# Attention, then experts: later waits for stores, the last normalisation on VectorE, shorter ranks and lists, products of ones in TensorE's waits

## What is computed

```python
x = x + attention(layernorm(x), ctx)     # self (causal) and cross, 16 heads, projection Wp
z = layernorm(x)
# expert choice: each of 8 experts takes the 512 of all 4096 tokens with the highest score
scores = (jnp.tanh(z @ gate_w.T) + 1.0) * 0.5
vals, idx = jax.lax.top_k(scores.T, 512)
y = layernorm(z[idx]) * gamma + beta
o = gelu(y @ fc1s + b1s) @ fc2s + b2s    # one 256 -> 1024 -> 256 network for each expert
out = x + z.at[idx].add(o * vals)
```

## Time and profile before

| | |
|---|---|
| time, median of 3 runs | 1618.84 us (1618.71, 1618.84, 1629.46) |
| the profiled execution's own time | 1623.42 us |
| its span, first to last instruction | 1621.7 us |
| PE, DVE, ACT, POOL busy | 92%, 70%, 56%, 34% of the span |
| mean granted clock | 0.95 |
| attention | to 1260 us, tail to 1281 us |
| routing, first list and first gather | 1281 to 1352 us |
| eight experts | 1352 us to the end |

### The profile page before, as it was taken

How to read it: one execution, slowest core, us unless ns; L and a number is a source line. 1 busy time by engine, 2 the same in 40 slices (tenths; PEclk the granted TensorE clock), 3 DMA queues, 4 the chain that set the end, 5 groups by cost and what they waited for, 6 DMA issues and landing times. The chain is left out here.

```text
span 1621.7 us, 26374 instructions
## 1 busy us (share of the span) xinstructions
PE 1486.5 (92%) x8925; PEld 726.8 (45%) x8925; DVE 1135.0 (70%) x3163; ACT 911.5 (56%) x1754; POOL 550.1 (34%) x1005
## 2 busy tenths in 40 slices
PE   8899999999999999999999999999998336999897
PEld 4443443444444444444444344444344223655564
DVE  6868887877887788778778887877850374554441
ACT  2167777677676777776776777777766001121111
POOL 4122333442352334334423533441131202434342
PEclk9599999999999999999999999999999557999999
DMA  6776652855467466728564773666001201443332
GB/s 131 153 137 104 128 81 81 114 117 103 103 115 126 94 93 127 124 79 116 104 116 100 113 130 83 102 122 108 4 3 40 83 1 53 92 114 98 105 87 50
DMA packets 82491, 155.46 MB, mean 96 GB/s; under 512 B 13012, under 2 KB 46420, under 8 KB 82356
## 3 DMA queue, kind: packets, MB, share of 16 engines
q1 hardware_dynamic: 76212, 145.25, 46.4%
q0 software_dynamic: 6144, 8.52, 3.0%
HBM read 96.52 MB, written 53.08 MB: 92 GB/s over the span
## 5 line engine op out<-in xcount | busy, mean ns | idle before, releaser
L827 ACT ACTIVATE probs<-bank_ps 128x512 f32<-128x512 f32 (+1 forms) x1408 | 730.4, 579 | 247.2 <-PE bank_ps L616 238.5
L918 DVE TENSOR_REDUCE chunk_max<-bank_ps 128x1 f32<-128x512 f32 x1024 | 653.5, 683 | 143.4 <-PE bank_ps L655 139.6
L655 PE MATMUL bank_ps<-k_stack,q_stack 62*128 62x512 f32 (+3 forms) x1536 | 536.1, 432 | 7.7 <-DVE chunk_max L918 4.4
L616 PE MATMUL bank_ps<-q_stack,k_stack 64*128 64x512 f32 (+3 forms) x1536 | 511.7, 422 | 26.0 <-ACT probs L827 22.6
L655 PEld LDWEIGHTS bank_ps<-k_stack,q_stack 62*128 62x128 f32 x1536 | 248.2, 191 | 371.3 <-DVE chunk_max L918 201.6
L921 DVE CUSTOM_DVE_ANT_0 masked<-bank_ps,causal 128x128 bf16<-128x128 f32 (+3 forms) x512 | 232.9, 485 | 62.1 <-PE bank_ps L655 58.6
L634 PE MATMUL out_ps<-probs,v_cross 128*32 128x512 f32 x2048 | 274.3, 608 | 0.0
L616 PEld LDWEIGHTS bank_ps<-q_stack,k_stack 64*128 64x128 f32 x1536 | 234.5, 189 | 83.9 <-ACT probs L827 76.5
L1081 POOL TENSOR_TENSOR pool_idle<-pool_idle 128x1 f32<-128x1 f32 x293 | 56.8, 194 | 581.9 <-ACT probs L827 383.5
L1379 ACT ACTIVATE h<-h_ps,b1T 128x512 f32<-128x512 f32 x64 | 44.0, 688 | 270.0 <-PE h_ps L1332 270.0
L1346 PE MATMUL o_ps<-w2T,h 128*128 128x256 f32 x512 | 117.1, 386 | 13.8 <-ACT h L1379 7.0
(11 more groups left out here) (159 smaller groups left out, 1357.1 us busy)
## 6 DMA issues: line engine op xcount, KB each, us to landing
parts_dram<-parts SPq DMA_DIRECT2D x70, 512.0 KB, 2.8
k_stack<-parts_dram SPq DMA_DIRECT2D x180, 192.0 KB, 11.7
q_stack<-parts_dram SPq DMA_DIRECT2D x180, 128.0 KB, 10.6
w1T<-in_L_ffn_fc1s SPq DMA_DIRECT2D x8, 1024.0 KB, 5.7
w2T<-in_L_ffn_fc2s SPq DMA_DIRECT2D x8, 1024.0 KB, 7.6
z_rows<-z_sb SPq DMA_DIRECT2D x8, 528.0 KB, 3.1
x_sb<-in_x SPq DMA_DIRECT2D x8, 512.0 KB, 3.9
ctxT<-in_ctx SPq DMA_DIRECT2D x8, 512.0 KB, 4.8
```

The source lines that it names most:

```text
L616: mm = pe.matmul(bank_of(turn)[:, of.at:of.end], k_stack[base:base + SIDE, g, pair, of.keys:of.keys + P], q_stack[base:base + SIDE, g, pai ...
L655: return pe.matmul(bank[:, 0:n], q_stack[base:base + MAX_ROWS, g, pair, qc:qc + P], k_stack[base:base + MAX_ROWS, g, pair, k0:k0 + n], sta ...
L827: nc.scalar.activation(probs[:, buffer(u, i, p), side, columns], bank_of(("score", g, i, p, side))[:, columns], ACT.Exp, scale=SCALE)\
L918: nc.vector.tensor_reduce(dst, bank[:, 0:n], AX.X, ALU.max).then_inc(max_done, 1)
```

## The change

`MEANWHILE` names four pieces of the last batch's tail behind which TensorE multiplies `ones_row` by itself into a bank that nobody reads (one 32-bit product of 512 columns, or four). VectorE takes the statistics of the first two tiles as soon as `proj0` is added, and normalises the last batch itself; POOL only makes `rstd` and the sum. `stored` is gone from the end of attention: `x1`, `z_sb` and the two semaphores outlive the block, and POOL waits for the stores ahead of the first gather (`z_out`) and the second (`base_out`). In the second block TensorE no longer waits for `consts` ahead of the rounds, and multiplies ones by `warm` (16-bit, 512 columns) four times behind each round and 32 times behind the first list. The ranks are counted from one; a third product with minus ones takes the subtraction's place; the tied tokens' counts have a bank of their own and don't wait for `count`; the last round makes no new levels, `thr` and `e_place` are not copied, `not_first` is set by POOL. `list_head` has 6 instructions. Each tile of a gather has its own semaphore.

```diff
+MEANWHILE = {"out_self": 1, "yT1": 1, "proj1": 4, "zT1": 1}
...
                 piece(epilogue_piece(B - 1, n), epilogue_bank(n))
+                if name in MEANWHILE:
+                    multiply_ones(MEANWHILE[name])
...
+                if name in PROJ_PIECES:
+                    c = PROJ_PIECES.index(name)
+                    dve.wait_ge(proj_added, 2 * B - 1 + c)
+                    tile_stats(1, x1[:, 2 * c, :], 2 * c)
+                    st = tile_stats(1, x1[:, 2 * c + 1, :], 2 * c + 1)
                 if name == "proj1":
-                    dve.wait_ge(proj_added, 2 * B)
-                    norm_stats(1, lambda t: x1[:, t, :], B)
+                    st.then_inc(stats_done[1], 1)
+                    mean_and_var(1, B)
+                    normalize(1, lambda t: z_sb[:, t, 0:C], lambda t: x1[:, t, :], B)
...
+                if n < B - 1:
+                    normalize(1, lambda t: z_sb[:, t, 0:C], lambda t: x1[:, t, :], n + 1)
+                else:
+                    deviation(1, n + 1)
...
-            stored(B)
...
-            pe.wait_ge(consts, 3)
+            def multiply_ones(times):
+
+                for _ in range(times):
+                    pe.matmul(transpose_ps[:, 0], ones[:], warm[:], start=True, stop=True)
+
+            pe.wait_ge(pool_set, 1)
             for r in range(ROUNDS):
                 pe.wait_ge(tested, r + 1)
                 for t in range(0, TILES, TILE_STEP):
                     mm = pe.matmul(reached_ps, ones[:], reached[:, :, :, t:t + TILE_STEP], start=t == 0,
                                    stop=t == TILES - TILE_STEP)
                 mm.then_inc(counted, 1)
-
-            pe.wait_ge(route, 2)
-            pe.matmul(count_ps[:, 0, :], ones[:], above[:].rearrange("p e t -> p (e t)"), start=True, stop=True)\
+                multiply_ones(ONES_PER_ROUND)
+
+            pe.wait_ge(consts, 3)
+            pe.wait_ge(route, 1)
+            pe.matmul(above_ps, ones[:], above[:].rearrange("p e t -> p (e t)"), start=True, stop=True)\
                 .then_inc(route_ps, 1)
-            pe.wait_ge(route, 4)
-            for n, tile in enumerate((tied, chosen)):
+            for tile, step in ((tied, 2), (chosen, CHOSEN_STEP)):
                 flat = tile[:].rearrange("p e t -> p (e t)")
-                if n:
-                    pe.wait_ge(route, CHOSEN_STEP)
-                pe.matmul(count_ps[:, 0, :], upto[:], flat, start=True, stop=True)
-                pe.matmul(count_ps[:, 1, :], ones[:], flat, start=True, stop=True).then_inc(route_ps, 1)
+                pe.wait_ge(route, step)
+                pe.matmul(count_ps[:], ones[:], flat, start=True, stop=True).then_inc(route_ps, 1)
+                pe.matmul(ahead_ps, upto[:], flat, start=True, stop=False)
+                pe.matmul(ahead_ps, minus_ones[:], flat, start=False, stop=True).then_inc(route_ps, 1)
             list_products(0)
+            multiply_ones(ONES_BEFORE_ITEMS)
...
-                nc.vector.tensor_copy(e_place[:], place[:, e, :])\
+                at = place[:, e, :]
+                nc.vector.tensor_tensor(e_at[:], at.unsqueeze(1).broadcast_to([P, NT + 1, TILES]),
+                                        chunk_from[:].unsqueeze(2).broadcast_to([P, NT + 1, TILES]), ALU.is_ge)\
                     .then_inc(list_step, 1)
                 dve.wait_ge(list_step, s + 1)
-                for c in range(1, NT):
-                    st = nc.vector.tensor_scalar(e_col[:, c, :], e_place[:], c * P - 0.5, None, ALU.is_ge)
+                nc.vector.tensor_reduce(e_sum[:], e_at[:, 1:NT, :].rearrange("p c t -> p t c"), AX.X, ALU.add)\
+                    .then_inc(list_step, 1)
+                nc.vector.tensor_tensor(e_col[:], e_at[:, 0:NT, :], e_at[:, 1:NT + 1, :], ALU.subtract).then_inc(list_step, 1)
+                dve.wait_ge(list_step, s + 2)
+                nc.vector.scalar_tensor_tensor(out=e_row[:], in0=e_sum[:], scalar=-float(P), in1=at,
+                                               op0=ALU.mult, op1=ALU.add).then_inc(list_step, 1)
+                dve.wait_ge(list_step, s + 3)
+                for v in range(2):
+                    st = nc.vector.tensor_tensor(e_rhs[:, :, v, :], e_col[:].rearrange("p c t -> p t c"),
+                                                 token[:, v, :].unsqueeze(2).broadcast_to([P, TILES, NT]), ALU.mult)
                 st.then_inc(list_step, 1)
...
+                dve.wait_ge(list_step, s + LIST_STEPS)
...
-                dve.wait_ge(rows_in, 16 * NT * (e + 1))
                 for t in range(NT):
+                    dve.wait_ge(rows_in[t], 16 * e + 16)
                     st = nc.vector.bn_stats(stats[:, t, :], rows[:, t, 0:C])
...
-                nc.vector.tensor_tensor(levels[:], low[:].unsqueeze(1).broadcast_to([P, 1 + TESTS, E]), steps[:],
-                                        ALU.add).then_inc(round_step, 1)
-
-            nc.vector.tensor_copy(thr[:], low[:]).then_inc(route, 1)
-            dve.wait_ge(route, 1)
-            nc.vector.tensor_tensor(above[:], s_all[:], wide(thr), ALU.is_gt).then_inc(route, 1)
-            nc.vector.tensor_tensor(tied[:], s_all[:], wide(thr), ALU.is_equal).then_inc(route, 1)
+                if r < ROUNDS - 1:
+                    nc.vector.tensor_tensor(levels[:], low[:].unsqueeze(1).broadcast_to([P, 1 + TESTS, E]), steps[:],
+                                            ALU.add).then_inc(round_step, 1)
+
+            nc.vector.tensor_tensor(above[:], s_all[:], wide(low), ALU.is_gt).then_inc(route, 1)
+            nc.vector.tensor_tensor(tied[:], s_all[:], wide(low), ALU.is_equal).then_inc(route, 1)
             dve.wait_ge(route_ps, 1)
-            nc.vector.tensor_reduce(count[:], count_ps[:, 0, :].rearrange("p (e t) -> p e t", e=E), AX.X, ALU.add)\
+            nc.vector.tensor_reduce(count[:], above_ps.rearrange("p (e t) -> p e t", e=E), AX.X, ALU.add)\
-            dve.wait_ge(route, 4)
+            dve.wait_ge(route, 3)
...
-            nc.vector.memset(not_first[:], 1.0).then_inc(route, 1)
-            dve.wait_ge(route, 6)
-            nc.vector.memset(not_first[:, :, 0:1], 0.0).then_inc(route, 1)
-            dve.wait_ge(route, 7)
+            dve.wait_ge(consts, 3)
...
                 dve.wait_ge(route, step + 1)
-                nc.vector.tensor_tensor(flat(tmp), flat(scan), count_ps[:, 1, :], ALU.subtract).then_inc(route, 1)
+                dve.wait_ge(route_ps, n + 1)
+                nc.vector.tensor_tensor(flat(place), flat(scan), ahead_ps, ALU.add).then_inc(route, 1)
                 dve.wait_ge(route, step + 2)
-                nc.vector.tensor_tensor(flat(place), flat(tmp), count_ps[:, 0, :], ALU.add).then_inc(route, 1)
-                dve.wait_ge(route, step + 3)
-
...
-CHOSEN_STEP = 13
+CHOSEN_STEP = 9
+ONES_PER_ROUND = 4
+ONES_BEFORE_ITEMS = 32
...
+            pool.wait_ge(z_out, 16 * BATCHES)
             gather(0)
+            pool.wait_ge(base_out, 16 * BATCHES)
```

101 lines of the change are left out of this document (49 added, 52 removed).

## The result

The changed kernel takes **1597.23 us** (median, 1593.62 to 1601.58, 4 runs), the kernel before 1621.99 (1618.71 to 1629.46, 4 runs). The ratio is 0.984, 95% interval 0.981 to 0.987: 1.6% faster. A second series gave 1592.72 (1591.76 to 1597.13, 5 runs) against 1624.18, ratio 0.982 (0.979 to 0.985). The prediction was 1594.7.

A forecast was written before the change was run, and what follows sets the result against it. Bound: the 80 us chain of attention's tail, routing and first gather, one engine at a time; in the experts, TensorE's waits. Terms sum to 25.1, 24.1 for the median: 1618.8 to 1594.7 us, own range 1590 to 1598, with rivals to 1602.

The forecast's parts named there:

- A: Tail of attention: earlier statistics, normalisation on VectorE, transposes and gate at the high clock; 6.7 us saved.
- B: Stores at attention's end: next block starts 0.44 behind the last store's issue, not its landing; 3.6 us (3.2 to 3.9).
- C: First round of the routing: TensorE no longer waits for POOL's last iota; 0.8 us (0.4 to 0.9).
- D: Routing rounds: four products of ones in each wait raise the clock and shorten the counting; 3.6 us (0 to 4.8).
- mostly high with a fall now and then: Granted clock expected in the 13 routing rounds, the first two low; basis for 3.6 us.
- ceiling of 4.8: Routing rounds: most gain if counting fell from 0.82 to 0.45, 0.37 a round, in all 13.
- Rival 1: Clock doesn't hold in the rounds nor first products: rounds give 0 to 1, gain 20.5, 1598 us; chance 0.20.
- E: Ranks and lists, last `low` to first one-hot: fewer and narrower VectorE operations; 4.0 us (3.0 to 5.0).
- F: First gather: three of four tile statistics now lie before the last landing; 1.0 us (0.4 to 1.1).
- the wait moves to POOL and covers itself: Stores: their wait, moved ahead of the first gather some 60 us later, was to cost nothing.
- G: 32 products of ones ahead of expert 0's transposes: transposes and first products run high; 0.5 us (-2.1 to 2.4).
- H: Experts: statistics by tile shorten TensorE's waits for VectorE, 6.6 us in 5 waits; 4.9 us (0.5 to 5.8).

The follow-up runs named there:

- undoing B alone: Changed kernel with SyncE again waiting for the last batch's two stores at attention's end and POOL's two waits gone: 1596.5 us, ratio 0.982.
- both experiments: Changed kernel with one wait for all four gathered tiles, 1599.5 us; kernel before with only a semaphore for each gathered tile, 1617.2 us.
- the second execution of before: The kernel before, unchanged, profiled once more: 1616.8 us, with 266.4 from the first product to the end.
- both ways of removing it: Changed kernel with stores waited for in attention, 1596.5 us; changed kernel with more ones, bridged, and POOL's waits ahead of its last iota, 1591.1 us.

## Why the prediction was right, point by point

- **Tail, stores, first round (A, B, C)**: 11.1 predicted, 11.15 measured (23.41 less 12.26), and 3.6 of it undone by undoing B alone. Durations of like instructions elsewhere in the trace were good to 0.03 us (transposes 1.06 for 1.09, gate 1.92 for 1.95, normalisation 1.38). The low case given for A is a slip: 6.7 less 1.6 is 5.1 and not 4.9. Not in the sum: the products ahead of the projection may also stop a fall of the clock that comes in some executions.
- **Rounds (D)**: this term was too large. In the profiled execution "mostly high with a fall now and then" failed: nine of 13 counts ran low, and it gained 1.2. In five others with the same rounds it gained 1.2 once and 2.9 four times; there it held, with three or four counts low. With four ones, and TensorE idle for 3.4 us or more ahead of them, the first two to four rounds are low; later the clock falls once in three of the six executions, twice in two and not at all in one. The ceiling of 4.8 was too high as well: all 13 rounds high give 3.9, 0.30 each, since the count took 0.51 and not the 0.45 that the gate's ratio gave. The Trainium skill ("TensorE: Matmul & The Clock Gate", section "A second HAM failure mode: psum-queue depth-cycling"), which the prediction weighed there, states that short idles between groups of products make the clock swing. Five of the six traces with four ones agree with it in kind, 0.50 and 1.00 in turn; the sixth, high for 23 us with 1.17 idle in every round, does not. Half of the ceiling, 2.4, lies inside what came. Rival 1, which gave D 0 to 1, came near twice in six. With seven ones the idles are still there, 0.53 a round, and the clock does not swing.
- **Ranks and lists (E)**: 4.1 for 4.0. Counting operations by width, 0.42, 0.29 and 0.16, was enough.
- **First gather (F)**: 0.4 for 1.0. The saving of three statistics is there (1.0 by both experiments); "the wait moves to POOL and covers itself" failed in a term of 0.36: a wait that is long satisfied, placed directly ahead of the gather, made its issue late. Another 0.15 goes with the wide operations on VectorE beside POOL's step (0.33 and not 0.19); with the wait still in place, undoing them alone brought 0.13, and only from the second transfer on.
- **Products ahead of the transposes (G)**: not late, as said; the fall of the clock in the gap behind them was named and came around the transposes each time. 0.2 here, and 0.5 in expert 0 (counted in H above), where 0.5 was put for both; expert 0 alone varies by more than that (33.0 and 33.9 in the two executions of the changed kernel).
- **Experts (H)**: the mechanism (VectorE free for tile 0 sooner) was right, the size in the profiled executions was not: 9.0 for 4.9. Against the second execution of before it is 6.2, and 5.3 in the second of the changed kernel, which is near 4.9; 2.8 was the first execution's own chance. What the term left out: "counts where TensorE waited" is too narrow, as an expert in which no wait for `o` shows became 0.35 shorter as well. The low clock behind the longest wait did go, but it was not there in the second execution of before either, so the change can't be given those 0.9.

The median came out at 1597.2 with 1594.7 predicted, inside the range. The gain of 24.8 (1621.99 less 1597.23) is close to the 24.1 put for the median, and that is in part luck: D and F were 3 us too hopeful and H up to 4 us too cautious, and the two offset each other. The time itself was missed by 2.5 us mostly through its anchor: 1618.84 is the median of three runs and lies 3 to 8 us below what more runs of before gave (1622.0, 1623.6, 1624.2, 1625.3, 1626.6). The 1 us taken off H for it was in the right place, as the first execution's experts were 2.8 us above the second's.

## What to carry to other kernels

In this chain, where one engine works at a time, a sum of durations from like rows elsewhere was good to 0.1 us a term (A, B, C and E); the clock and the landings of transfers are not in that sum, and take a second profile of the kernel before to know their chance. Where products of ones are to hold the clock, size them to the wait at the *high* clock, not to the one at the low: four fitted the wait at the low clock, left 1.17 of 2.55 us idle at the high one, and in five executions of six it fell again; seven, which left 0.53, kept it in three of three. When whole times scatter more than the effect, measure from the last point that the change does not touch.

## What was not expected of the hardware

- The granted clock went to and fro in the rounds with four products of ones (TensorE 80 to 85% busy before it rose, 55% before it fell), but in one execution of six it stayed at 1.00 for 23 us with the same 54%. With seven it stayed at 1.00. Why the same rounds swing in one execution and not in another is open.
- Being late was cheap: eight ones cost 0.6 us in one round, once, and the rounds were as short as with four or shorter.
- POOL's first gather came 0.36 us later behind a second wait that had long been satisfied (POOL idled 47 us for the other), and 0.15 later beside wide operations of VectorE. That the wait's place is the cause of the 0.36 is shown by both ways of removing it; why it costs anything is open.
- Attention, the same instructions up to its tail, took 1255.7 to 1262.8 us from execution to execution, by falls of the clock of 3.4 or 6.8 us that came in different batches.
